# A wait before every gather of a graph layer, instead of before every eighth

## What is computed

```
h = emb; acc = emb
for _ in range(2):
    h = segment_sum(adj_val[:, None] * h[adj_col], adj_row, num_segments=N)
    acc = acc + h
graph_item_embs = acc / 3
combined = graph_item_embs[items] + item_features[items]
seq_hidden = take_along_axis(combined, alias_inputs[..., None], axis=1)
...                       # tanh, sigmoid, attention weights over 50 items
scores = 12 * l2norm(sess_emb) @ l2norm(graph_item_embs).T
```

## Time and profile before

| | us |
|---|---|
| median of 3 runs | 4842.74 |
| the three runs | 4837.10, 4842.74, 4855.09 |
| the profiled execution | 4823.57 |
| its span, first to last instruction | 4821.8 |
| first layer, first gather to last add | 759.3 to 2549.3 |
| second layer, first gather to last add | 2576.2 to 4361.8 |

### The profile page before, as it was taken

The page is one execution under the profiler, slowest core; times in us unless marked ns, Lnnn a source line. Parts: engine busy times, 40 slices in busy tenths (PEclk is TensorE's granted clock), DMA queues, the critical chain, the costliest instruction groups (busy, mean ns, idle before and its releaser), DMA issues.

```text
span 4821.8 us, 44188 instructions
## 1 busy us (share of the span) xinstructions
PE 2980.1 (62%) x9770; PEld 1769.6 (37%) x9770; DVE 2997.7 (62%) x7246; ACT 870.3 (18%) x3004; POOL 2969.9 (62%) x3059
## 2 busy tenths in 40 slices
PE   4989884555555555555565555555565555554688
PEld 2777772233333232332232233322232323232344
DVE  8999994556656565565564565555565556555355
ACT  1998991000000000000000000000000000005343
POOL 1566666666666666666664666666666666664650
PEclk8888886666766676667766776676676777766789
DMA  0000001111111111111114111111111111134363
GB/s 31 3 3 3 3 3 44 46 45 46 46 45 46 46 46 46 45 46 46 46 46 141 44 47 45 46 46 46 45 46 45 46 47 45 46 100 84 42 115 141
DMA packets 140023, 234.88 MB, mean 49 GB/s; under 512 B 56500, under 2 KB 84080, under 8 KB 139760
## 3 DMA queue, kind: packets, MB, share of 16 engines
q0 software_dynamic: 95904, 177.31, 15.8%
q1 hardware_dynamic: 41476, 55.61, 3.4%
q10 hardware_dynamic: 2508, 0.60, 0.1%
HBM read 192.37 MB, written 41.01 MB: 48 GB/s over the span
## 4 chain that ended last, share of the span: by engine, by line
POOL 39%; issue 21%; another core or an unknown queue 15%; DVE 14%; PE 7%; ACT 3%; DVEq 1%; DMA 1%; ACTq 0%; SPq 0%; POOLq 0%
POOL ring L522 38%; DVE acc L1086 5%; ACT big L592 2%; PE bank L1438 2%; DVE stage L873 1%; PE bank L1466 1%; DVE ring L1037 1%; DVE big L817 1%; PE bank L1425 1%; PE bank L1299 1%; DVE ring L825 1%; DVE big L833 1%; POOL sorted_edges L492 1%; DVE stage L898 1%
## 5 line engine op out<-in xcount | busy, mean ns | idle before, releaser
L1362 PE MATMUL bank<-ring 128*128 128x256 f32 x4968 | 2029.6, 533 | 1541.9 <-DVE ring L1037 911.9
L1362 PEld LDWEIGHTS bank<-ring 128*128 128x128 f32 x4968 | 1066.6, 248 | 2488.2 <-DVE ring L1037 1382.5
L1086 DVE TENSOR_TENSOR acc<-acc,bank 128x256 f32 x2484 | 1048.6, 422 | 1457.1 <-remote 1129.0
L522 POOL DMA_INDIRECT ring<-table,cring x1242 | 1174.7, 946 | 639.5 <-issue 362.0
L522 POOL DMA_INDIRECT ring<-in_L_rec_emb,cring x1242 | 1175.9, 947 | 608.1 <-issue 365.6
L1037 DVE TENSOR_SCALAR ring<-bank,mlo,mval 128x256 f32<-128x256 f32 x2484 | 1360.6, 548 | 30.5 <-DMA ring<-table,cring 19.1
L608 ACT COPY mlo<-ring 128x24 f32 (+1 forms) x104 | 22.1, 212 | 3350.6 <-PE bank L1362 1652.5
L592 ACT ACTIVATE big<-big 128x68 f32<-128x68 bf16 x1764 | 558.8, 410 | 1.3 <-issue 1.1
L1299 PE MATMUL bank<-big,ring 128*128 128x136 f32 x2352 | 432.7, 327 | 78.5 <-issue 18.8
L492 POOL DMA_INDIRECT sorted_edges<-moved,block_to x313 | 392.9, 1255 | 102.0 <-issue 102.0
L1299 PEld LDWEIGHTS bank<-big,ring 128*128 128x128 f32 x2352 | 355.9, 218 | 153.2 <-ACT big L592 90.8
(11 more groups left out here) (209 smaller groups left out, 1617.2 us busy)
## 6 DMA issues: line engine op xcount, KB each, us to landing
scores<-stage SPq DMA_DIRECT2D x48, 512.0 KB
ring<-in_L_rec_emb,cring POOLq DMA_INDIRECT x1242
ring<-table,cring POOLq DMA_INDIRECT x1242
table<-big SPq DMA_DIRECT2D x7, 896.0 KB, 8.4
combined<-ring SPq DMA_DIRECT2D x7, 896.0 KB, 7.4
sorted_edges<-moved,block_to POOLq DMA_INDIRECT x313
ring<-combined,sidi POOLq DMA_INDIRECT x200
sorted_edges<-ring SPq DMA_DIRECT2D x1, 1248.0 KB, 4.4
```

The source lines that it names most:

```text
L522: pool.indirect_dma_start(msg[:, s, :], None, source, bass.IndirectOffsetOnAxis(cring[:, s:s + 1], 0)).then_inc(s_g[s], 16)
L1086: add = dve.tensor_tensor(acc[:, bass.ds(off, BUCKET)], acc[:, bass.ds(off, BUCKET)], bank[u % PR][:, 0:BUCKET], ALU.add)
L1362: pe.matmul(bank[u % PR][:, 0:BUCKET], msg[:, h * T + u, :], onehot[:, u % SR, :], start=True, stop=True).then_inc(s_mm[u % M], 1)
```

## The change

The number PACE goes. The test for every eighth gather goes with it, so each gather waits for the product of the twelfth tile before it. Gathers then run at most 12 tiles ahead of the last finished product, at all times. Nothing else differs: the same gathers, slots, semaphores and values.

```diff
-    PACE, AHEAD = 8, 12
+    AHEAD = 12
...
                     s = h * T + u
-                    if u % PACE == 0:
-                        done = NU * layer + T * c + u - AHEAD
-                        if done > 0:
-                            pool.wait_ge(s_mm[(done - 1) % M], (done - 1) // M + 1)
+                    done = NU * layer + T * c + u - AHEAD
+                    if done > 0:
+                        pool.wait_ge(s_mm[(done - 1) % M], (done - 1) // M + 1)
                     pool.indirect_dma_start(msg[:, s, :], None, source,
                                             bass.IndirectOffsetOnAxis(cring[:, s:s + 1], 0)).then_inc(s_g[s], 16)
```

## The result

The changed kernel takes **4819.98 us** (median of 7 runs, 4816.52 to 4826.09), the kernel before 4842.74 (7 runs beside them, 4835.07 to 4857.69). The medians are 22.8 us apart. The ratio, after over before, is 0.9956, with a 95% interval of 0.9944 to 0.9968, so 0.44% faster. The part ahead of the prediction has it the other way round.) The time lies in the forecast range, and 22.8 us is just within what the prediction called the same (0.5%, 24 us). But the forecast was no gain, and the interval leaves no doubt that this is one. Its profiled execution is 4816.52 us.

What follows compares the result with a forecast made beforehand. Gathers on POOL, at 1.25 us each plus 0.18 us of pauses, were taken to set the pace. Profiled 4823.6 + 0 (waits) + 2 (restarts) = 4826 us, or 4845 as a median; range 4785 to 4950.

Steps and rivals of the forecast that it cites:

- The beat, 1.25 us a gather: On POOL, a gather takes 947 ns plus 0.30 us between two; 1242 of them make 1553 us of a layer's 1785.
- Waits that are satisfied cost nothing: On POOL's gathers, an already satisfied wait adds 0; upper bound 0.01 us x 2174 new waits = 22 us.
- Where the new waits hold: Only inside spells, stopping POOL at 12 tiles ahead; stretches of 16 to 20 gathers between pauses.
- spells: Periods in which TensorE's products are executed but reported slowly, one in 3 to 5 us, until POOL has stood still.
- the place at 887.7: Trace point with 92 gathers and 80 adds begun; gather 93 would wait until 890.8, a pause of 3.1 us.
- debt: Each tile leaves 0.18 us of work somewhere, paid while POOL pauses, in however many pieces; chance 0.56.
- rival A: Short POOL pauses don't pay, so time in them is lost: 87 to 174 us slower, 4930 to 5020 us; chance 0.25.
- rival B: Spells end because POOL stands still at all, so shorter pauses do: 62 to 110 us faster, 4735 to 4780; chance 0.15.
- What that is worth: Gain from POOL's earlier stops: nothing by the debt, ±21 us; +2 us taken for some ten more stretches.
- Cover that goes: Less lead hides the gathers' flight; VectorE's wait for their data left at 19.1 + 7.5 us, ±10 us for both layers.
- The clock: More gaps between TensorE's products could lower its clock; slower products are hidden by 1541.9 us of PE idleness, so no term.
- The spread: The whole kernel's time, eight in ten: 4785 to 4950 us, taking in the nearer half of A and near end of B.

Runs made afterwards that it cites:

- again3: The changed kernel once more, on a chip where the kernel before takes 4290.17 or 4296.60 us and has no late reports; ratio to it 1.0002.
- again2: The changed kernel run once more, on the same chip as null2; ratio to the kernel before 0.9959.
- again: The changed kernel run once more, on another chip than again2; ratio to the kernel before 0.9942.
- pace2: The changed kernel with a wait at each second gather only (PACE 2, AHEAD 12); ratio to the kernel before 0.9936.
- null: The kernel before, unchanged, run again as a yardstick; ratio 0.9996, median 4850.54 us.
- null2: The kernel before, unchanged, run again on another chip than null; ratio 1.0007, median 4848.14 us.
- pace12: The kernel with a wait at each twelfth gather only (PACE 12, AHEAD 12); 5075.87 us, ratio to the kernel before 1.0470.
- ahead8: The changed kernel with each gather waiting for the product of the eighth tile before it (AHEAD 8); ratio to the kernel before 0.9948.

## Why the prediction was wrong

**The beat, 1.25 us a gather:** right, 942 to 947 ns and 0.30 us on every chip. On two of them it is the whole layer.

**Waits that are satisfied cost nothing:** right. again3 has 2161 more waits than the kernel before (the prediction's 2174 counts the first gathers, which have none) and the same time, within 0.1%. The bound of 22 us can go.

**Where the new waits hold:** right in kind. Long pauses restart 12 ahead (62 of 63 in again2), and spells are cut earlier; but there were 404 waits for late products, not 150 to 300, as many spells are now broken by several short pauses. Between two pauses of over 2 us POOL makes 37 gathers on average, not 14 to 20. One slip was in the count: at AHEAD 12 gather 93 waits for product 80, not 81, so the place at 887.7 would have stopped POOL one gather later than I wrote.

**Short pauses pay the debt (against rival A):** right. With 401 such waits (again) or 178 (pace2) the idle time is the same to 3 us. Rival A's sum over 520 us did not come. Nor did rival B's under 380. The forecast of 430 to 460 us came true (452.4 in the profile after), but by luck: it was taken from a profile with a cheaper debt, and the loss that the change ends made up for it.

**"What that is worth":** this is the step that failed, in its first words, "By the debt, nothing", and in the term "I take +2 us, for some ten more stretches at most with a tenth or two lost at a restart". I gave the restart loss to the *new* kernel, some ten times. It belongs to the *old* one: 0.5 us at each of the 46 long pauses that end at a round's first gather, 25 us, against 3 to 7 such pauses in the new one. In place of +2 us, POOL's idle time fell by 24 us (null to again) and 29 us (null2 to again2). I had it in my rows: the stretch of 24 gathers that took 34.6 us ends at the 265th gather, a round's first; those of 16 that took 22.9 and 22.8 us do not the earlier trace rows. I called the difference between 1.442 and 1.425 us a gather the spread of the rows. The stretches of 24 that end elsewhere take 34.21 us in that trace, 1.425 again. The restart at 897.20 is a round's first too, the 97th gather, 1.5 us behind the last late add. I looked at what the new waits stop, and not at how the old ones let go.

**Its base** was one execution, and an odd one. The loss at rounds' first gathers is in it like in the others (49 long pauses, 0.50 us each). What it has less of is the debt: 0.176 us a gather in the stretches that end elsewhere, against 0.188 in null and null2. So the profiles before and after, laid side by side, hid the gain. The sum was made against that execution's 4823.6 us and moved to the median by adding 19 us, as if nothing of the kernel's stages hung on it. Why it differs is open; its sort, too, was 9 us shorter than theirs.

**Cover that goes:** right, one-hots waited 31.0 us, forecast under 60.

**The clock:** the new kernel's clock in the layers is 0.67 where null2 has 0.69 and 0.70, and a pass of PE lasts longer, as the product's rows of null2 and again2 show:

```profile
L1362 PE MATMUL bank<-ring 128*128 128x256 f32 x4968 | 2010.7, 530 | 1578.1 <-DVE ring L1037 960.9
```

```profile
L1361 PE MATMUL bank<-ring 128*128 128x256 f32 x4968 | 2149.7, 564 | 1404.9 <-DVE ring L1036 976.2
```

The Trainium skill (TensorE: Matmul & The Clock Gate, section "Why this matters for your kernels") says that gaps between bursts bring the clock down. The mean clocks here don't show it: PE is idle for 173 us less before its products in again2 than in null2, with fewer gaps of over 2 us (279 against 333), and its clock is lower; pace12 has the most idleness (1829.8 us) and 0.69 and 0.71. What brought the clock from 0.69 to 0.67 is open. The layers are shorter all the same, as PE still has 1404.9 us of idleness before its products. To give the clock no term was right.

**The spread:** 4785 to 4950 held the time. But it was centred on a base that counted as typical and was not; and no case of mine had a gain of 0.4% by a mechanism of its own.

## What to carry to other kernels

A coarse wait (one in n, on a counter that runs) costs at the restart, not while it holds, so read the restarts one by one: the time from the report to the instruction that it releases, and the place of that instruction in its loop. Here it was 0.26 us, but 0.76 where a second wait stood at the same place, the head of a round, and one wait in three of the kernel before stood there. How many products past the late one the wait asks for cost nothing while these were already made, and became dear from the point where the awaited work itself stands behind the waiting queue's consumers (here six products on, by LEAD: 4.7% slower). And when the profiled execution lies outside the runs, find out in which term it differs before any other term is sized from it; and when two groups of rows differ by 0.5 us in a steady way, look for what divides them before calling it spread.

## What the runs showed of the hardware that I had not expected

- **Chips differ by 12% on one program.** Medians of the kernel before were 4852.19, 4846.02 and 4806.73 us on three chips, and 4290.17 and 4296.60 on two others. In the layers all of it is TensorE's reports coming late: 483 us more idle time before gathers in null2 than in again3. But the sort (768.7 to 743.3 us) and the part behind the layers (448.8 to 400.8) are shorter too. What makes the difference is open; the granted clock in the layers is no higher on the quick chips (0.65 and 0.70).
- **Reports of products can be late by microseconds, in spells.** In null2 adds stood 4.71 and 3.33 us for products that were made but not reported, until POOL had been still for some 4 us. Perfetto Trace Analysis of the Trainium skill, section "Tensor Engine Instruction (MATMUL, LD_WEIGHTS)", has the semaphore update pushed when PSUM acknowledges that all bytes are written. On the two quick chips the trace has nothing between (0.01 to 0.02 us from a product's end to its report), on two of the other three they lie far apart: 19 us in the case shown above, and late adds begin up to 23 us after the end of their product in null2. What holds the report back was not found: no run on a chip with spells had the size of gather or product changed beside its base.
- **The debt is nearly conserved.** The pauses of the kernels with a wait at each gather or each second one are 450.6 to 460.8 us in sum on two of the chips that have it, 0.181 to 0.186 us a gather, whether the kernel waits 178 or 426 times for a late product; in ahead8, on the third, 434.9.
- **A gather starts 0.26 us after the report it waits for, or 0.76 us,** the latter at a round's first gather, where a separate wait instruction stands before it (null2: 90 and 46 waits). A queue that works ahead hides the difference: with the report already there, both have 0.30 us before them.
